# Last turn of a two-layer graph kernel: its output path cut into two halves of 256 columns

## What is computed

```python
Wh = einsum('bni,hoi->bhno', h, W) + bW
e = einsum('bhno,hop->bhnp', Wh, attn)
A_mat = tanh(where(adj, einsum('bhnp,bhmp->bhnm', e, Wh), 0))
hp = relu(einsum('bhnm,bhmo->bhno', A_mat, Wh))
cat = hp transposed and reshaped to (graph, node, 4 * 256)
ha = cat @ A_w.T
hf = h @ fc_w.T
coeff = sigmoid(hf @ g1_w.T + ha @ g2_w.T + gbias)
out = layernorm(h + hf * coeff + ha * (1 - coeff))
```

## Time and profile before

| | us |
|---|---|
| median of 3 runs | 1116.5 (1112.35 to 1117.24) |
| profiled execution, its own time | 1114.91 |
| its span in the profile | 1113.1 |
| busy TensorE | 1090.0 |
| busy DVE | 711.7 |
| busy ACT | 542.1 |
| mean granted TensorE clock | 0.992 of 2.4 GHz |

### The profile page before, as it was taken

How to read it: one execution, slowest core, us unless ns; L and a number is a source line. 1 busy time by engine, 2 the same in 40 slices (tenths; PEclk the granted TensorE clock), 3 DMA queues, 4 the chain that set the end, 5 groups by cost and what they waited for, 6 DMA issues and landing times.

```text
span 1113.1 us, 25068 instructions
## 1 busy us (share of the span) xinstructions
PE 1090.0 (98%) x10018; PEld 911.4 (82%) x10018; DVE 711.7 (64%) x1353; ACT 542.1 (49%) x958; POOL 281.3 (25%) x247
## 2 busy tenths in 40 slices
PE   7999999999999999999999999999999999999995
PEld 5878888888888888888888888888788888888774
DVE  6666765757666666765757666575765666676543
ACT  3654463635536364563735546363563635445351
POOL 1533222232312313222232312213221231322200
PEclk8999999999999999999999999999999999999998
DMA  7000100001010000100001010000100100010000
GB/s 258 2 22 22 40 23 21 19 21 39 21 38 22 20 19 21 39 21 20 22 20 37 21 39 21 20 19 21 39 21 20 40 20 19 21 40 3 1 19 19
DMA packets 26699, 32.58 MB, mean 29 GB/s; under 512 B 4400, under 2 KB 23344, under 8 KB 26288
## 3 DMA queue, kind: packets, MB, share of 16 engines
q1 hardware_dynamic: 26672, 32.19, 8.6%
HBM read 23.80 MB, written 8.39 MB: 29 GB/s over the span
## 4 chain that ended last, share of the span: by engine, by line
PE 96%; DVE 1%; DMA 1%; ACT 1%; issue 0%; SPq 0%; POOL 0%; POOLq 0%; DVEq 0%
PE bank L380 17%; PE bank L381 17%; PE bank L385 17%; PE bank L372 8%; PE bank L374 8%; PE bank L373 8%; PE bank L575 5%; PE bank L598 4%; PE bank L489 3%; PE bank L502 3%; PE bank L520 2%; PE bank L645 1%; PE bank L545 1%; PE bank L408 1%; DMA bias_v<-in_bv 1%; PE bank L420 1%
## 5 line engine op out<-in xcount | busy, mean ns | idle before, releaser
L840 ACT ACTIVATE cat_hi<-bank 128x512 fp32r<-128x512 f32 x128 | 76.6, 598 | 127.0 <-PE bank L385 127.0
L805 ACT ACTIVATE T<-bank 128x512 f32<-128x512 f32 x128 | 76.6, 599 | 102.6 <-PE bank L385 100.8
L936 DVE SCALAR_TENSOR_TENSOR cat_lo<-bank,cat_hi 128x512 fp32r<-128x512 f32 x128 | 86.5, 686 | 38.9 <-ACT cat_hi L840 36.8
L936 DVE SCALAR_TENSOR_TENSOR U_lo<-bank,U_hi 128x512 fp32r<-128x512 f32 x128 | 78.0, 682 | 50.5 <-ACT U_hi L834 50.5
L380 PE MATMUL bank<-hT_hi,g_lo 128*128 128x512 f32 x256 | 102.9, 402 | 0.0
L381 PE MATMUL bank<-hT_hi,g_hi 128*128 128x512 f32 x256 | 99.9, 390 | 0.0
L381 PE MATMUL bank<-U_hi,wt_hi 128*128 128x512 f32 x256 | 99.8, 390 | 0.0
L380 PE MATMUL bank<-U_hi,wt_lo 128*128 128x512 f32 x256 | 99.8, 390 | 0.0
L372 PE MATMUL bank<-cat_lo,aw_hi 128*128 128x512 f32 x256 | 99.6, 389 | 0.0
L373 PE MATMUL bank<-cat_hi,aw_lo 128*128 128x512 f32 x256 | 99.6, 389 | 0.0
L374 PE MATMUL bank<-cat_hi,aw_hi 128*128 128x512 f32 x256 | 99.6, 389 | 0.0
(11 more groups left out here) (154 smaller groups left out, 2743.3 us busy)
## 6 DMA issues: line engine op xcount, KB each, us to landing
y<-in_x SPq DMA_DIRECT2D x16, 512.0 KB, 3.6
out<-res SPq DMA_DIRECT2D x16, 512.0 KB, 3.0
x_raw<-in_xT SPq DMA_DIRECT2D x15, 512.0 KB, 3.3
W_nat<-in_Wn SPq DMA_DIRECT2D x1, 1028.0 KB, 6.1
attn_nat<-in_attn SPq DMA_DIRECT2D x1, 1024.0 KB, 8.6
adjS_u<-in_adjS SPq DMA_DIRECT2D x32, 32.0 KB, 2.7
raw_A<-in_AwT SPq DMA_DIRECT2D x1, 1024.0 KB, 8.0
x_second<-in_xT SPq DMA_DIRECT2D x1, 512.0 KB, 9.6
```

Source lines behind the costliest of these rows:

```text
L805: take(act.activation(T[:, n % DC, n // DC, :], bank[:], ACT.Copy), "B", f"T{n}", g)
L840: act.activation(cat_hi[:, n, :], bank[:], ACT.Relu).then_inc(cat_hi_ready, 1)
L936: return dve.scalar_tensor_tensor(out=out, in0=bank, scalar=bias, in1=hi.bitcast(F32), op0=op, op1=ALU.subtract)
```

## The change

In the last turn alone, what follows the cat tiles is done in two halves of the columns (s = 0: columns 0 to 255, s = 1: the rest), by new functions whose names end in `_half`. Matmuls, ACT and DVE operations have 256 columns in place of 512, and there are twice as many; the gate's products over h come in halves too, each in its own bank (four banks z00 to z11 in place of two). TensorE's order is: ha of half 0 (c = 0, 1), half 1 (c = 0), gate of half 0, half 1 (c = 1), transposes of half 0, gate of half 1, transposes of half 1. DVE takes statistics and normalizes straight from the bank of the transposes; ACT's copy to `res` is gone for group 15. POOL takes the root of each half, and SP stores each half with a DMA of its own. `h_a_half(g, 0, 0)` waits for all eight cat tiles before it claims its bank. The cat tiles rotate through four banks. The transposes of group 14, and ACT's copies of them, come after the fourth T tile and not after the second.

The diff, without lines of context:

```diff
@@ -50,9 +50,9 @@
-LAST = listed("T0:4 T1:5 Rp0:0 Rp1:1 T2:6 T3:7 T4:4 T5:5 T6:6 T7:7 hf0:4 adj0:5 adj1:6 hf1:2 U000:7 U001:4 U010:5 U011:6 "
-              "U100:0 U101:1 U110:3 U111:2 z0:7 z1:4 cat0:5 cat1:6 cat2:0 cat3:1 cat4:3 cat5:2 cat6:5 cat7:6 "
-              "ha0:0 ha1:1 R0:2 R1:3")
+LAST = listed("T0:4 T1:5 T2:6 T3:7 Rp0:0 Rp1:1 T4:4 T5:5 T6:6 T7:7 hf0:4 adj0:5 adj1:6 hf1:2 U000:7 U001:4 U010:5 U011:6 "
+              "U100:0 U101:1 U110:3 U111:2 z00:7 z01:4 z10:5 z11:6 cat0:0 cat1:1 cat2:3 cat3:2 cat4:0 cat5:1 cat6:3 cat7:2 "
+              "ha00:0 ha01:1 ha10:3 ha11:2 R0:7 R1:4")
@@ -271,6 +271,10 @@
+        def half_cols(t, s):
+            return t[:, s * D:s * D + D]
         def of_graph(t, c, b):
@@ -363,8 +367,12 @@
             whole(sp, turn)
-            store(GROUPS - 1)
-            sp.wait_ge(stored, 16 * GROUPS)
+            for s in range(2):
+                sp.wait_ge(out_ready, (GROUPS - 1) * NP + 2 * s + 2)
+                sp.dma_start(out[GROUPS - 1, 2 * s:2 * s + 2].rearrange("p t d -> t p d"),
+                             res[:, 2 * s:2 * s + 2, :]).then_inc(stored, 16)
+            sp.wait_ge(stored, 16 * (GROUPS + 1))
         def _(pe):
@@ -635,6 +643,44 @@
+            def gate_h_half(g, s):
+                for c in range(DC):
+                    bank = claim(pe, "B", f"z{s}{c}", g)
+                    dense(bank[:, 0:D], [
+                        (FF, (hT_hi, hT_lo), lambda t, k=k: t[:, k, D + c * P:D + c * P + P],
+                         lambda t, k=k: of_graph(t, k, s))
+                        for k in range(DC)], last=False)
+            def h_a_half(g, s, c):
+                if not (s or c):
+                    for k in range(KC):
+                        await_taken(pe, "B", f"cat{k}", g)
+                bank = claim(pe, "B", f"ha{s}{c}", g)
+                for k in range(KC):
+                    ins = product(bank[:, 0:D], Aw, (cat_hi, cat_lo), lambda t: t[:, k, c * P:c * P + P],
+                                  lambda t: half_cols(t[:, k, :], s), k == 0, k == KC - 1)
+                filled(ins, "B", f"ha{s}{c}", g)
+            def gate_a_half(g, s):
+                for k in range(DC):
+                    pe.wait_ge(haT_ready, g * DC + 2 * s + k + 1)
+                    for c in range(DC):
+                        ins = product(bank_of("B", f"z{s}{c}", g)[:, 0:D], G2, (haT_hi, haT_lo),
+                                      lambda t: t[:, k, c * P:c * P + P], lambda t: half_cols(t[:, k, :], s),
+                                      False, k == DC - 1)
+                        if k == DC - 1:
+                            filled(ins, "B", f"z{s}{c}", g)
+            def res_T_half(g, s):
+                pe.wait_ge(resT_ready, g * DC + 2 * s + 2)
+                bank = claim(pe, "B", f"R{s}", g)
+                for q in range(2):
+                    for c in range(DC):
+                        ins = pe.transpose(bank[:, q * D + c * P:q * D + c * P + P],
+                                           tile_cols(rT[:, c, :], 2 * s + q), ident[:])
+                filled(ins, "B", f"R{s}", g)
             def res_T(g):
@@ -674,18 +720,24 @@
-                    if A is None and n == 1:
+                    if A is None and n == 3:
                 if A is None:
-                    gate_h(B)
+                    for s in range(2):
+                        gate_h_half(B, s)
                     heads_out(B, range(KC))
-                    h_a(B)
-                    gate_a(B)
-                    res_T(B)
+                    h_a_half(B, 0, 0)
+                    h_a_half(B, 0, 1)
+                    h_a_half(B, 1, 0)
+                    gate_a_half(B, 0)
+                    h_a_half(B, 1, 1)
+                    res_T_half(B, 0)
+                    gate_a_half(B, 1)
+                    res_T_half(B, 1)
@@ -849,6 +901,16 @@
+            def h_a_half(g, s, c):
+                bank = await_tile(act, "B", f"ha{s}{c}", g)
+                act.activation(half_cols(haT_hi[:, c, :], s), bank[:, 0:D], ACT.Copy).then_inc(haT_hi_ready, 1)
+            def gate_half(g, s):
+                for c in range(DC):
+                    bank = await_tile(act, "B", f"z{s}{c}", g)
+                    ins = act.activation(half_cols(th[:, c, :], s), bank[:, 0:D], ACT.Tanh, scale=0.5)
+                    take(ins, "B", f"z{s}{c}", g)
             def res_out(g):
@@ -905,9 +967,12 @@
-                    h_a(B)
-                    gate(B)
-                    res_out(B)
+                    h_a_half(B, 0, 0)
+                    h_a_half(B, 0, 1)
+                    h_a_half(B, 1, 0)
+                    gate_half(B, 0)
+                    h_a_half(B, 1, 1)
+                    gate_half(B, 1)
@@ -1115,6 +1180,46 @@
+            def h_a_half(g, s, c):
+                bank = bank_of("B", f"ha{s}{c}", g)[:, 0:D]
+                dve.wait_ge(haT_hi_ready, g * DC + 2 * s + c + 1)
+                low(half_cols(haT_lo[:, c, :], s), bank, half_cols(haT_hi[:, c, :], s)).then_inc(haT_ready, 1)
+                await_taken(dve, "B", f"hf{c}", g)
+                part = half_cols(hf[:, c, :], s)
+                dve.tensor_tensor(part, part, bank, ALU.subtract)
+                new = half_cols(rT[:, c, :], s).rearrange("p (q n) -> p q n", q=NP)
+                take(dve.tensor_tensor(new, of_graph(hT, c, s), bank.rearrange("p (q n) -> p q n", q=NP), ALU.add),
+                     "B", f"ha{s}{c}", g)
+            def gated_half(g, s):
+                for c in range(DC):
+                    e, r = half_cols(hf[:, c, :], s), half_cols(rT[:, c, :], s)
+                    await_taken(dve, "B", f"ha{s}{c}", g)
+                    await_taken(dve, "B", f"z{s}{c}", g)
+                    dve.scalar_tensor_tensor(out=e, in0=half_cols(th[:, c, :], s), scalar=1.0, in1=e,
+                                             op0=ALU.add, op1=ALU.mult).then_inc(e_ready, 1)
+                    dve.wait_ge(e_ready, g * DC + 2 * s + c + 1)
+                    dve.scalar_tensor_tensor(out=r, in0=e, scalar=0.5, in1=r, op0=ALU.mult, op1=ALU.add) \
+                       .then_inc(resT_ready, 1)
+            def moments_half(g, s):
+                bank = await_tile(dve, "B", f"R{s}", g)
+                for q in range(2):
+                    dve.bn_stats(stats2[:, 2 * s + q, :], bank[:, q * D:q * D + D]).then_inc(stats2_ready, 1)
+                for q in range(2):
+                    dve.wait_ge(stats2_ready, g * NP + 2 * s + q + 1)
+                    dve.bn_aggr(mv2[:, 2 * s + q, :], stats2[:, 2 * s + q, :]).then_inc(mv2_ready, 1)
+            def normalized_half(g, s):
+                dve.wait_ge(rstd2_ready, g + s + 1)
+                dve.wait_ge(stored, g * 16)
+                bank = bank_of("B", f"R{s}", g)
+                for q in range(2):
+                    p = 2 * s + q
+                    dve.tensor_scalar(res[:, p, :], bank[:, q * D:q * D + D], mv2[:, p, 0:1], rstd2[:, p:p + 1],
+                                      ALU.subtract, ALU.mult).then_inc(out_ready, 1)
             def result_moments(g):
@@ -1163,9 +1268,16 @@
                 if A is None:
-                    for c in range(DC):
-                        h_a(B, c)
-                    gated(B)
+                    h_a_half(B, 0, 0)
+                    h_a_half(B, 0, 1)
+                    h_a_half(B, 1, 0)
+                    gated_half(B, 0)
+                    h_a_half(B, 1, 1)
+                    moments_half(B, 0)
+                    gated_half(B, 1)
+                    normalized_half(B, 0)
+                    moments_half(B, 1)
+                    normalized_half(B, 1)
@@ -1181,8 +1293,6 @@
             whole(dve, turn)
-            result_moments(GROUPS - 1)
-            result_normalized(GROUPS - 1)
         def _(pool):
@@ -1250,6 +1360,13 @@
+            def root_half(g, s):
+                part = slice(2 * s, 2 * s + 2)
+                pool.wait_ge(mv2_ready, g * NP + 2 * s + 2)
+                pool.tensor_scalar(rstd2[:, part], mv2[:, part, 1], EPS, None, ALU.add).then_inc(root2, 1)
+                pool.wait_ge(root2, g + s + 1)
+                pool.tensor_tensor(rstd2[:, part], rstd2[:, part], half[:, part], ALU.pow).then_inc(rstd2_ready, 1)
             def turn(A, B, more):
@@ -1280,7 +1397,8 @@
                     hT_whole(A)
             whole(pool, turn)
-            root_2(GROUPS - 1)
+            for s in range(2):
+                root_half(GROUPS - 1, s)
```

## The result

| | before | after |
|---|---|---|
| median of 13 runs, us | 1115.0 (1112.35 to 1117.24) | 1111.03 (1109.28 to 1112.69) |
| ratio | | 0.9961, 95% interval 0.9952 to 0.9970 |
| span of the profiled execution, us | 1113.1 | 1110.2 |

The change makes the kernel faster by 0.39%, 4.3 us (4.0 by the medians); the forecast was 3.1 us, within 0.5%.

The account below looks back on a forecast made before the run. TensorE was taken as the bound (96% of the chain that ended last). The last store 2.9 us earlier, all terms included, and 0.2 from its landing gave -3.1: 1116.5 to 1113.4 us; own range 1112 to 1115, whole 1109.5 to 1116.5.

Parts of the forecast that it names:

- the last rival: End of the kernel: last transposes stay at 2.4 GHz, last store lands by its bytes; gain 4.8 us, 1111.7; chance 0.13.
- Head, -1.43: Start of the last turn: TensorE's wait for rT of group 14 goes, 1.43 us less.
- Gate over h in halves, +0.16: Gate products over h: 24 of 256 columns replace 12 of 512, 2.88 us against 2.72, 0.16 more.
- Products over cat, +0.64: Products over cat: 96 of 256 columns replace 48 of 512, 11.52 us against 10.88, 0.64 more.
- the gate ahead, +1.44: TensorE: 12 gate products of half 0 stand ahead of the last ha half, 1.44 us more.
- The new wait, +1.65: Before the first product over cat: TensorE waits for all eight cat tiles, 1.65 us more.
- The tail, from last product to store: After the last product over cat: work in halves shrinks the way to the store from 14.1 to 8.85 us.
- The last store, -0.2: End of the kernel: the last store, now 256 KB, lands 0.2 us sooner; 1.5 in proportion to bytes as other bound.
- POOL did not hold DVE: Rival, tail: POOL's root of half 0 holds DVE's gated half 1; up to 1.0 us more, 1114.4; chance 0.08.
- Half-size instructions: Rival, tail: they cost nearly whole ones, 0.25 us more each for eight; gain 1.1, 1115.4; chance 0.05.
- The clock did not fall at the new wait: Rival, products after the cat wait: TensorE's clock falls, up to 14.4 us more, 1127.8, slower; chance 0.04.
- the fourth rival: End of the kernel: transposes at full clock (0.4 us) and store landing by bytes (1.3 more); gain 4.8; chance 0.13.

Follow-up runs that it names:

- e2: Kernel before, with only the transposes of group 14 and their ACT copies moved behind the fourth T tile; ratio to the kernel before 0.9983.
- e1: Changed kernel with the wait for each cat tile put back right before the first product with that tile; ratio to the kernel before 0.9947.
- e10: Changed kernel with the bank of ha claimed ahead of the eight waits for cat tiles; first product over cat 0.15 us after DVE's last low part.
- e11: Changed kernel profiled once more, unchanged; 61.10 us from the last turn's first T0 product to the span's end, against 61.40 in its first profile.
- e8: Changed kernel with POOL's last root (half 1) taken over all four columns instead of two; ratio 0.9966.
- e4: Changed kernel with one store of 512 KB for the last group instead of two of 256 KB; ratio 0.9967.
- e5: Changed kernel with DVE's tail reordered: gated half 1 first, then both halves' moments, then both normalizations; ratio 0.9974.
- e7: Changed kernel with ACT's copies to res put back in halves, DVE's statistics and normalization reading res; ratio 0.9971.

## Why the prediction was right

Its sign, its mechanism and its most costly item were right; the gain was 4.0 us in the profile (4.3 in the timed runs) where it said 3.1. The time itself is a looser hit. 1113.4 was forecast and 1111.0 measured: 1.5 of these 2.4 us are the base (a median of 1116.5 over three runs, 1115.0 over thirteen), and the rest is the gain. 1111.0 lies in the whole range (1109.5 to 1116.5), which was widened for such scatter, but outside the forecast's own (1112 to 1115), nearest to the last rival (1111.7).

*Head, -1.43.* Measured -1.46 (e2). *Gate over h in halves, +0.16.* e1 has the first product over cat at 35.64, the head alone at 35.49: +0.15. *Products over cat, +0.64, and the gate ahead, +1.44.* From the start of the first product to that of the last, e1 (no wait there) takes 12.83 us and the kernel before 10.65: +2.18 against the sum's +2.08; 0.1 of that is the last slot, which counting from start to start leaves out.

*The new wait, +1.65.* Measured 1.85 (e1). The rows named give 1.52 + 0.06 + 0.11 = 1.69, not 1.65; the trace after gives 1.52 + 0.25 + 0.08. The step that was too small is the hand-over from DVE, 0.25: 0.06 was taken from a wait with nothing behind it; here the claim's wait stands behind (0.10 of it, e10), and 0.09 stays open.

*The tail, from last product to store.* Counted from the start of that product: before 14.47; said 9.13; measured 8.51, or 8.27 at the full clock (e11). Against e11: the statistics-to-aggregates wait of 0.14 was not there with two in place of four, twice; the wait for the root was taken as 1.57 and was 1.15 (0.33 of that by its two columns less, e8); the transposes were taken at half the clock, 0.87, and took 0.66 (0.97 in the profile after, and 1.10 near half the clock, e8). Against that, the normalization from the bank cost 0.26 more for two: over the 0.1 allowed for each, inside the 0.4 for all four reads. The 0.2 that remains lies in DVE's steps ahead of the gated half, which follow each other more closely than they were summed.

*The last store, -0.2.* The term that was mis-sized most: 0.8 (e4). The 2.8 us of the row for 256 KB is a load of the prologue; a store of 256 KB lands in 2.1. Why the load takes longer, no run shows. The proportion of bytes (1.5), held as the other bound, was as far off on the other side.

The rivals: POOL did not hold DVE, whose gated operations beside the power took 0.41 to 0.42 us. POOL's two took 0.32 and 0.86 there, against 0.23 and 0.71 with DVE idle; in e5 the power of half 1 (1106.32) took 0.71 beside a normalization that reads the bank. The Trainium skill ("SBUF — State Buffer", SBUF: two separate sides) has the later of the two wait for the whole instruction of the other. The trace agrees only in part: POOL, which began later (1102.33 against 1102.19), was the slower, but DVE's next operation began at 1102.53, inside POOL's 0.86 us, and took 0.42 like the others. No run here separates the causes. Half-size instructions cost 0.38 and 0.42, as in the prologue. The clock did not fall at the new wait: the products behind it keep 0.12 us, with a granted clock of 1.00 from 1086.20 to 1099.10. Of what the fourth rival named, the store is 0.6 us of the 0.9 by which the profile beat the forecast. The clock is none of it there, since it had fallen as forecast; in the repetition, where it held, it adds 0.2.

## What to carry over

Splitting the end of a kernel into halves pays by what overlaps, and the price is on the same path: here 2.2 us of narrower and reordered products and 1.85 us of a wait that was gathered at the front of the first half, against 6.0 us off the tail behind the last of these products. No run has the halves' overlap alone; of the tail, e7 puts 0.3 us on reading the bank and e8 0.3 on the narrower root, and the rest is put down to the overlap. A wait belongs right before the instruction that needs it. When a change is worth a few us in a thousand, read it from a fixed point just before it in the profile: the anchored readings repeat to 0.02 us, the start of the last turn scatters by 4.

## What was not expected of the hardware

The last store: 2.1 us to landing for 256 KB, 2.9 for 512. DVE's two-scalar normalization: 1.00 us for two of 128x256 from a bank, 0.73 from SBUF, while two statistics cost the same from either (0.76, 0.75). POOL's power: 0.71 us for two columns, 1.04 for four. The granted clock: behind equal waits of 2.15 us it held at 2.4 GHz in five profiles and fell in three; what decides between the two stays open.
